# Attention scores from 32-row groups of q and k in a two-layer gated block on one Trainium2 core

## The reference

```python
def _L0_xattn_ref(x, context, w_qkv, w_proj, b_proj):   # 16 heads of width 8
    qkv = (x @ w_qkv.T).reshape(B, N, 3, H, D).transpose(2, 0, 3, 1, 4)
    q, k, v = (qkv[0], qkv[1], qkv[2])
    kv = context.reshape(B, N_c, 2, H, D).transpose(2, 0, 3, 1, 4)
    extra_k, extra_v = (kv[0], kv[1])
    k = jnp.concatenate([extra_k, k], axis=2)
    v = jnp.concatenate([extra_v, v], axis=2)
    attn = jax.nn.softmax(jnp.einsum('bhnd,bhmd->bhnm', q * scale, k), axis=-1)
    out = jnp.einsum('bhnm,bhmd->bhnd', attn, v)
    return out.transpose(0, 2, 1, 3).reshape(B, N, C) @ w_proj.T + b_proj
...
x = x + tanh(g_xattn[0]) * L0_xattn(layernorm(x), ctx)
x = x + tanh(g_ffn[0]) * L0_ffn(layernorm(x))        # one shared and one of 8 routed experts
x = x + tanh(g_xattn[1]) * L1_xattn(layernorm(x), ctx)
x = x + tanh(g_ffn[1]) * L1_ffn(layernorm(x))        # two of 8 experts
```

## Time and profile before

| | us |
|---|---|
| median of 3 runs | 590.63 (590.25 to 591.71) |
| profiled execution | 596.14 |
| its span, first to last instruction | 593.7 |
| PE busy | 516.4, 87% of the span |
| DVE busy | 411.6, 69% |
| ACT busy | 310.4, 52% |
| POOL busy | 274.4, 46% |
| mean granted clock of TensorE | 0.954 of full |

### The profile page before, as it was taken

The page is one execution under the profiler, slowest core; times in us unless marked ns, Lnnn a source line. Parts: engine busy times, 40 slices in busy tenths (PEclk is TensorE's granted clock), DMA queues, the critical chain, the costliest instruction groups (busy, mean ns, idle before and its releaser), DMA issues. The chain is left out here.

```text
span 593.7 us, 19118 instructions
## 1 busy us (share of the span) xinstructions
PE 516.4 (87%) x5902; PEld 365.0 (61%) x5903; DVE 411.6 (69%) x1348; ACT 310.4 (52%) x843; POOL 274.4 (46%) x693
## 2 busy tenths in 40 slices
PE   1789999999999999987927699997676789999998
PEld 0456666666666666654523355554444579999997
DVE  3888888898988888833374344542445589999974
ACT  2477777777777777652313456652333244444420
POOL 5545544465556555554320100006542588887520
PEclk9899999999999999988966899997989889999999
DMA  7900120000000000000011612221000001111000
GB/s 269 378 16 21 35 122 4 3 12 12 10 9 9 9 10 9 12 17 13 19 54 32 126 44 63 68 69 39 25 9 6 9 26 39 36 36 31 19 19 27
DMA packets 24215, 26.24 MB, mean 44 GB/s; under 512 B 4969, under 2 KB 21153, under 8 KB 23521
## 3 DMA queue, kind: packets, MB, share of 16 engines
q1 hardware_dynamic: 20688, 15.31, 8.4%
q0 software_dynamic: 3472, 10.26, 5.9%
HBM read 17.50 MB, written 7.91 MB: 43 GB/s over the span
## 5 line engine op out<-in xcount | busy, mean ns | idle before, releaser
L892 DVE TENSOR_REDUCE negm<-PS 128x4 f16<-128x512 f32 x128 | 84.7, 684 | 1.0 <-PE PS L1236 0.8
L651 ACT ACTIVATE pexp<-PS 128x512 f32<-128x512 f32 x128 | 78.3, 619 | 9.1 <-PE PS L1249 9.1
L1548 PE MATMUL PS<-w,vp 128*128 128x128 f32 x512 | 63.1, 277 | 0.0
L1548 PEld LDWEIGHTS PS<-w,vp 128*128 128x128 f32 x512 | 60.3, 193 | 0.1
L1236 PE MATMUL PS<-ktp,arena 128*64 128x128 f16 x1024 | 53.2, 227 | 4.7 <-DVE negm L892 3.5
L1263 PE MATMUL PS<-pexp,vp 128*32 128x64 f32 x2048 | 54.5, 227 | 2.1 <-ACT pexp L651 0.8
L1099 DVE SCALAR_TENSOR_TENSOR pexp<-PS,xs,oS 128x256 f32<-128x256 f32 x40 | 19.4, 484 | 50.5 <-ACT oS L752 47.5
L1449 PE MATMUL PS<-rgu,xsT 128*128 x80 | 48.4, 689 | 4.4 <-ACT xsT L757 2.6
L1236 PEld LDWEIGHTS PS<-ktp,arena 128*64 128x64 f16 x1024 | 33.0, 110 | 26.3 <-issue 15.0
L1263 PEld LDWEIGHTS PS<-pexp,vp 128*32 128x32 f32 x2048 | 34.8, 110 | 22.1 <-issue 11.7
L484 POOL TENSOR_TENSOR ve<-mv,epsc 128x1 f32<-128x1 f32 x32 | 6.1, 192 | 90.3 <-DVE mv L928 90.3
(11 more groups left out here) (225 smaller groups left out, 1317.5 us busy)
## 6 DMA issues: line engine op xcount, KB each, us to landing
xs<-sorted_x SPq DMA_DIRECT2D x40, 64.5 KB, 1.8
sorted_y<-YS SPq DMA_DIRECT2D x40, 64.0 KB, 1.6
arena<-mT SPq DMA_DIRECT2D x128, 1.0 KB
rgu<-in_rt_gate_up_dram POOLq DMA_DIRECT2D x1, 2048.0 KB, 8.0
out_dram<-X SPq DMA_DIRECT2D x32, 64.0 KB, 1.6
X<-in_x_dram SPq DMA_DIRECT2D x1, 1536.0 KB, 8.5
CK<-in_ctx_k_dram SPq DMA_DIRECT2D x1, 1536.0 KB, 11.7
CV<-in_ctx_v_swapped_dram SPq DMA_DIRECT2D x1, 1536.0 KB, 15.8
```

The costliest lines, as they stand in the source:

```text
L651: nc.scalar.activation(pexp[:, j, :], PS[:, 2 + j % 2, :], ACT.Exp).then_inc(S["exped"], 1)
L892: dve.tensor_reduce(negm[:, a.par, :, j], PS[:, j % 2, :].rearrange("p (h k) -> p h k", h=HG), AX.X, ALU.max, negate=True).then_inc(S["max ...
L1548: nc.tensor.matmul(PS[:, 6 + y.par, 0:D], z[:, y.par, e, :], w1[:, e * D:e * D + D], start=(e == 0), stop=False)
```

## The change

The block-diagonal q is gone. The scores are made from 32 rows of `qc` and the same 32 rows of `kt` by matmuls that use one 32-row group of the array; consecutive matmuls alternate between two row groups, hg = 2 half and 2 half + 1, and between two banks. A chunk (one bank, one maximum, one exponential) is now one `hg` over all groups and, in the second scores, both sequences. The first scores come in two halves of 16 matmuls, the second in two halves of 16 matmuls with 64 elements streamed. Both banks of a half are released and filled together. The order on PE changes with it; those on ACT, DVE and SP stay, except that the four L939 instructions and the waits for them are gone. The averages of a bank are laid out by `hg`, so the normalisation reads and writes with other strides.

```diff
-        qc = sb("qc", [P, G, P], F16)
+        qc = sb("qc", [P, 4, G, P], F16)
...
-                        sp.dma_start(qbd[32 * hg + 24:32 * hg + 25, a.slot, :, hg, :],
+                        sp.dma_start(qc[32 * hg + 24:32 * hg + 25, a.slot, :, :],
...
-                    act.wait_ge(S["q_spread"], s.freed(back=1))
...
-                if s:
-                    for hg in range(HG):
-                        last = dve.tensor_scalar(qbd[:, s.slot, :, hg, :], qc[:], in_group[:, hg:hg + 1], None, ALU.mult)
-                    last.then_inc(S["q_spread"], 1)
...
+            def scores_for_max(a, half):
+                if half == 0:
+                    pe.wait_ge(S["q_kept"], a.done())
                     pe.wait_ge(S["k_kept"], a.done())
                     pe.wait_ge(S["ctx_kept"], a.done())
+                pe.wait_ge(S["maxed"], a.freed(4, 2 * half + 1, back=2))
+                for g in range(G):
                     for b in range(2):
+                        for hg in (2 * half, 2 * half + 1):
+                            rows = slice(32 * hg, 32 * hg + 32)
+                            last = nc.tensor.matmul(PS[64 * b:64 * b + 64, hg % 2, g * P:g * P + P],
+                                                    qc[rows, a.slot, g, 64 * b:64 * b + 64], kt[rows, a.slot, b, g, :],
+                                                    start=True, stop=True)
+                            if (g, b) == (G - 1, 1):
+                                last.then_inc(S["scored"], 1)
...
+            def scores_by_key(b, half):
+                if half == 0:
                     pe.wait_ge(shift_placed[b.par], 64 * (b.pair + 1))
+                pe.wait_ge(S["exped"], b.freed(4, 2 * half + 1, back=2))
+                for seq in range(2):
+                    for g in range(G):
+                        for hg in (2 * half, 2 * half + 1):
+                            rows = slice(32 * hg, 32 * hg + 32)
+                            at = (seq * G + g) * SEQ
+                            last = nc.tensor.matmul(PS[:, 2 + hg % 2, at:at + SEQ], kt[rows, b.slot, seq, g, :],
+                                                    qc[rows, b.slot, g, SEQ * seq:SEQ * seq + SEQ], start=True, stop=True)
...
                     nc.tensor.transpose(PS[:, 6, 0:P], on[:, m.par, :], identf).then_inc(S["on_turned"], 1)
-                if a:
-                    scores_for_max(a, 1)
+                if b:
+                    scores_by_key(b, 0)
...
-                if b:
-                    scores_by_key(b, 0)
-                    scores_by_key(b, 1)
...
                 if a:
-                    scores_for_max(a, 2)
+                    scores_for_max(a, 1)
...
                 if b:
                     average(b, 0)
+                    scores_by_key(b, 1)
+                    average(b, 1)
                 if f:
                     pe.wait_ge(S["xnT_kept"], f.done())
                     nc.tensor.matmul(PS[:, 4, P:4 * P], xnT[:, f.par, :], wqkv[:], start=True, stop=True)\
                         .then_inc(S["qkv_done"], 1)
-                if b:
-                    scores_by_key(b, 2)
-                if b:
-                    average(b, 1)
-                    scores_by_key(b, 3)
-                if a:
-                    scores_for_max(a, 3)
```

More of the change, by code:

```diff
@@ L134, in flamingo_gated_two_layers @@
         VALL = sb("VALL", [P, NT * DW])
-        CW = [P, P, P, P, E, E, NS, 1, SEQ, TURN * E, HG]
+        CW = [P, P, P, P, E, E, NS, 1, SEQ, TURN * E]
         CO = [sum(CW[:i]) for i in range(len(CW))]
         cst = sb("cst", [P, sum(CW)])
-        identf, upper, ones, decay, exp_no, exp_no8, tile_start, patch_no, place_no, regions, in_group = (
+        identf, upper, ones, decay, exp_no, exp_no8, tile_start, patch_no, place_no, regions = (
             cst[:, o:o + w] for o, w in zip(CO, CW))
@@ L891, in max_chunk @@
                 dve.wait_ge(S["scored"], a.done(4, j))
[L892 removed]
+                dve.tensor_reduce(negm[:, a.par, :, j], PS[:, j % 2, :].rearrange("p (g k) -> p g k", g=G),
                                   AX.X, ALU.max, negate=True).then_inc(S["maxed"], 1)
@@ L1225, in _ @@
             pe.wait_ge(pool_consts, 2)
-            def scores_for_max(a, j):
-                if j == 0:
-                    pe.wait_ge(S["q_spread"], a.done())
+            def scores_for_max(a, half):
+                if half == 0:
+                    pe.wait_ge(S["q_kept"], a.done())
                     pe.wait_ge(S["k_kept"], a.done())
                     pe.wait_ge(S["ctx_kept"], a.done())
-                pe.wait_ge(S["maxed"], a.freed(4, j, back=2))
-                for hg in range(HG):
+                pe.wait_ge(S["maxed"], a.freed(4, 2 * half + 1, back=2))
+                for g in range(G):
@@ L1235, in scores_for_max @@
                     for b in range(2):
[L1236 to L1243, removed]
-                    pe.wait_ge(shift_placed[b.par], 64 * (b.pair + 1))
[L1245 to L1251, removed]
+                        for hg in (2 * half, 2 * half + 1):
[5 more added lines that the diff above has]
+                                last.then_inc(S["scored"], 1)
@@ new lines, in scores_by_key @@
+            def scores_by_key(b, half):
+                if half == 0:
+                    pe.wait_ge(shift_placed[b.par], 64 * (b.pair + 1))
+                pe.wait_ge(S["exped"], b.freed(4, 2 * half + 1, back=2))
[6 more added lines that the diff above has]
+                                                    qc[rows, b.slot, g, SEQ * seq:SEQ * seq + SEQ], start=True, stop=True)
+                            if (seq, g) == (1, G - 1):
+                                last.then_inc(S["scored_t"], 1)
@@ L1258, in average @@
                 pe.wait_ge(S["exped"], b.done(4, j))
[L1259 to L1265, removed]
+                for seq in range(2):
+                    for g in range(G):
+                        last = nc.tensor.matmul(PS[32 * g:32 * g + 32, 7, j * P + SEQ * seq:j * P + SEQ * seq + SEQ],
+                                                vp[:, b.par, seq, g * HG + j, :],
+                                                pexp[:, j, (seq * G + g) * SEQ:(seq * G + g + 1) * SEQ],
                                                 start=True, stop=True)
@@ L1575, in constants @@
                           + [np.broadcast_to(r, (P, r.size)) for r in rows]
-                          + [p[:, None] % 64, np.broadcast_to(np.arange(64), (P, 64)), region, p[:, None] // 32 == np.arange(4)], 1).astype(np.float32)
+                          + [p[:, None] % 64, np.broadcast_to(np.arange(64), (P, 64)), region], 1).astype(np.float32)
 def kernel(**inputs):
```

17 lines of the change are left out of this document (8 added, 9 removed).

## The result

| | before | changed |
|---|---|---|
| median, us | 591.17 (590.25 to 596.27, 4 runs) | 685.87 (679.96 to 697.82, 4 runs) |
| ratio to before | 1 | 1.153 (95%: 1.144 to 1.162) |
| profiled: span, us | 593.7 | 677.9 |
| PE busy, us | 516.4 | 569.2 |
| DVE busy, us | 411.6 | 377.3 |

A forecast was written before the change was run, and what follows sets the result against it. Bound: PE's work ahead of qkv, ACT's chain to exp 3 behind it. 28 steps x 0.53 = 14.8, drain 1.6, first tile 1: +17.4 us, median 590.63 to 608; own range 602 to 614, whole range 602 to 631.

The forecast's parts named there:

- the rival on the clock: Attention stage: a few drops to the half level, 1.5 us each, add 4 to 15 us, giving 612 to 623; chance 0.12.
- a clock below 1.00 in the steady stage: Steady attention stage: a granted clock under 1.00 was listed as a sign that the forecast is wrong.
- the first tile: First tile: its key half waits for the maxima's DMA and later PE work queues behind it, 1 us once.
- Ahead of qkv: Step start to qkv matmul: PE work +0.25 us plus an `xrT` wait; qkv starts at 4.43, not 4.00 us.
- Max halves: First scores, 16 matmuls per half: row groups run side by side, four passes, 0.35 us per half.
- key halves: Second scores, 16 matmuls of 64 elements per half: side by side with hidden weight loads, 0.34 us per half.
- Behind qkv: From qkv to step end: stays 3.50 us because of ACT's order; 1.34 us of removed work becomes waiting.
- The first rival: Whole step: PE's work is the bound, so -1.1 us per step over 28 steps, 560 us; chance 0.05.
- The second rival: Score halves: row groups do not run side by side, 0.56 us per half, +19 us, 627; chance 0.18.
- fourth rival: Key halves: 32-row weight loads are slower, a half takes 1.0 us, +36 us, 645 or more; chance 0.06.
- DMA of the maxima: First key half of a step: the DMA it needs stays hidden, with 0.4 us in hand.
- DVE's spreading: DVE, beside PE's work: removing 1.20 us of busy time per tile is worth nothing.

The follow-up runs named there:

- e3: Kernel before with score matmuls from 32 rows, no block-diagonal q, PE's order of before, row groups not interleaved: 754.6 us, ratio 1.275.
- e2: Kernel before (block-diagonal q, 128 rows) with only PE's order of the changed kernel: 626.3 us, ratio 1.058.
- e11: Changed kernel plus 13 filler matmuls of 32 rows x 128 columns ahead of averages 2 and 3: 677.0 us, ratio 1.140 to the kernel before.
- e4: Changed kernel with ACT's and DVE's orders fitted to PE's, exp 2 and 3 ahead of the cast: 592.9 us, ratio 1.000 to the kernel before.
- e10: e4 with the first key half moved behind the turns on PE: 580.1 us, ratio 0.972 to the kernel before.
- e13: Changed kernel plus 6 filler matmuls of 128 rows x 128 columns ahead of averages 2 and 3: 616.8 us, ratio 1.039 to the kernel before.
- e14: The same kernel as e10, run again: 582.7 us, ratio 0.976 to the kernel before.
- e7: Kernel before with the first scores alone from 32 rows, second scores from the block-diagonal q: 599.6 us, ratio 1.012.
- e8: Kernel before with the second scores alone from 32 rows, first scores from the block-diagonal q: 606.6 us, ratio 1.024.

## Why the prediction was wrong

- **The step that failed is the clock.** The sum took over the clock of 1.00 from the earlier trace rows as if it belonged to the stage, and the rival on the clock was priced as "a few such drops in the stage, 1.5 us each, give +4 to +15", by the share of waiting time read from the earlier trace rows, with a chance of 0.12. The runs put nearly all of the miss there: 685.9 us for the changed kernel, 616.8 when six 128-row matmuls in its wait hold the clock, 69 us. The prediction named "a clock below 1.00 in the steady stage" as a sign of being wrong, and that sign came. Two things were wrong in the price. The busy share was taken for what the clock follows, though the change cuts the rows in use to a quarter in every score matmul; e3, busy all the time, is at half clock, e2, waiting as much as the changed kernel, is at 0.97. And a drop was taken to be short; under thin work it lasts (e3 from 27 us to the end of its stage, e11 for 102 us).
- **It took both parts of the change together.** Its order alone, with the waits and all 128 rows, gives 626 (e2). The interleaved thin matmuls without the long waits give 593 (e4) and 580 (e10). With the waits they give 686.
- **The rest of the sum.** With the clock held in the stage, the ratio is 1.039 (1.029 to 1.049), +23 us; forecast +17.4. Four steps of e13, from qkv to qkv, take 32.9 us (7.94 + 8.69 + 8.00 + 8.27), 2.2 more than before; forecast 2.1. That this came out is no luck: the parts of the step came out as well. The term that was too small is the first tile, which was estimated at 1 us. The first average of the run and the first matmul of the sorted experts, in the kernel before (L1263, L1449) and in e13:

```profile
33.94 0.43 PE L1263 MATMUL PS<-pexp,vp 128*32 128x64 f32 x16
314.65 2.07 PE L1449 MATMUL PS<-rgu,xsT 128*128 x2 [0.88 <-ACT xsT L757]
...
37.52 0.66 PE L1262 MATMUL PS<-pexp,vp 128*32 128x64 f32 x16
336.20 2.07 PE L1443 MATMUL PS<-rgu,xsT 128*128 x2 [0.87 <-ACT xsT L755]
```

The first average comes 3.6 us later, and its matmuls still have the lengths of the half level, so part of that is the clock again. From there to the last qkv (237.16 and 256.64 us) it is 15.9 us more, for 14.8 forecast, and from the last qkv to the sorted experts 2.1, for 1.6. Together 21.6.

- **Ahead of qkv:** 4.51 us against 4.43. Max halves 0.35 and key halves 0.34 are exact; `xrT` waited 0.18, as worked out, and gained 0.
- **Behind qkv:** 3.50 us, and nothing of the 1.34 us taken out was gained. The waits in front of the averages (0.96 and 0.40) are that time. e4 shows the cause by removing it: with exp 2 and 3 ahead of the cast the same PE list takes 6.9 us a step for about 8. The first rival (PE's work is the bound, 560) needs ACT and DVE reordered as well, and then it comes near for the steps (6.5 to 7.1 us in e4, e10 and e14), not for the clock or the time (580 to 593).
- **The second rival** (row groups do not run side by side) did not come true; they do: 16 matmuls of 128 elements from two row groups and two column halves in 0.35 us with the change of shape is four passes, not eight, and in each half matmuls of two row groups start within 0.01 us of each other. The overhead of 60 cycles a matmul that the Trainium skill gives (TensorEngine Tiling (Array Packing), Instruction Overhead) does not agree with it: it made 0.53 us of a half that took 0.34.
- **Weight loads of 32 rows** (fourth rival) cost nothing that shows: a key half with 16 of them takes 0.34, as worked out with those in the earlier trace rows.
- **DMA of the maxima:** no wait for it in the steady stage of the changed kernel, as forecast. In e4, with steps of 6.9 us, its 0.4 us of cover is gone (from 120 to 240 us PE waits for it ten times, 2.7 us in all): moving the key half behind the turns (e10) then took 0.3 us off the step.
- **DVE's spreading:** DVE's busy time falls from 411.6 to 377.3 us. That this is worth nothing by itself, as forecast, fits the steps, but no run takes out the spreading alone.

What stays open: where between one and two of the thin scores the clock gives way (e7 and e8 hold, e3 doesn't), whether e3's work would also have lost a full clock, what starts the single drops in e4 to e14, and why the fall in e11 came when it did.

## What to carry to other kernels

Before cutting a matmul to fewer rows, ask what it does to TensorE's clock: the array time saved is no gain if the stage drops to 1.2 GHz, and here a block diagonal of which three quarters are zero held the clock at 1.00 where the same products from 32 rows did not. Moving or shortening work on the busiest engine gives nothing behind a point where another engine's order sets the pace; change both orders or neither. Read the granted clock of each stage first, beside the length of a matmul that both kernels have, and when a stage becomes thinner by rows or waits more, take the half level as a case of its own, for the whole stage, and not as a few drops.

## What the runs showed of the hardware that was not expected

- Granted clock 0.50 for 352 us on end with PE busy 351.04 us of them, in a stage whose score matmuls use 32 rows (e3).
- The same idle time filled with matmuls of equal number and elements: 128 rows x 32 columns 1.00; 64 rows x 128 columns 1.00, 1.00, 0.88; 32 rows x 128 columns 1.00, 0.81, 0.50. It is rows that count here, not cells (128 x 32 and 32 x 128 are as many, 64 x 128 twice as many).
- The two levels hold themselves: the kernel with thin fillers ran 96 us at the full and then 102 us at the half level, with the same instructions in every four steps (7.6 to 8.4 us a step, then 13.4 to 13.6).
- The recorded clock can read 1.00 early in a trace where qkv has the length of the half level, 1.59 us for 0.91 (e13, 27 to 42 us), and a recorded mean of 0.961 stood beside an execution as long as one with 0.699 (e3).
- Matmuls in two row groups and two column halves run side by side: 16 of 128 elements with 16 weight loads in 0.35 us, the changes of the array's shape included.
